# Table look-up of the feed-forward weights: products on POOL, sums on DVE

## The reference, cut to what matters

```python
xn = layernorm(x)                                     # (1, 1024, 256)
# attention: 16 heads of 128, causal, with a distance bias per head
q, k, v = split(xn @ qkv_w + qkv_b)
attn = softmax(q @ k.T + alibi_mask)
a = (attn @ v) @ out_w + out_b
# feed-forward: the weights are indices into a table of 16 values
gate = xn @ lut[gate_idx].T                           # gate_idx, up_idx: (688, 256)
up = xn @ lut[up_idx].T
f = (silu(gate) * up) @ lut[down_idx].T               # down_idx: (256, 688)
return x + a + f
```

## Time and profile before

| | us |
|---|---|
| median of 3 runs | 543.18 |
| lowest, highest | 539.96, 543.33 |
| profiled execution, device time | 543.26 |
| profiled execution, span of the core's instructions | 541.5 |
| PE busy | 493.8 (91%) |
| DVE busy | 414.2 (76%) |
| POOL busy | 403.6 (75%) |
| ACT busy | 360.9 (67%) |
| DMA queue that moves all data, share of 16 engines | 30.2% |

### The profile page before, as it was taken

How to read it: one execution, slowest core, us unless ns; L and a number is a source line. 1 busy time by engine, 2 the same in 40 slices (tenths; PEclk the granted TensorE clock), 3 DMA queues, 4 the chain that set the end, 5 groups by cost and what they waited for, 6 DMA issues and landing times.

```text
span 541.5 us, 9700 instructions
## 1 busy us (share of the span) xinstructions
PE 493.8 (91%) x2826; PEld 422.4 (78%) x2826; DVE 414.2 (76%) x1067; ACT 360.9 (67%) x657; POOL 403.6 (75%) x312
## 2 busy tenths in 40 slices
PE   7896797999889988998899989997999989789998
PEld 6785576898779876987689768986798779578897
DVE  6796988788888878888788987888788886543541
ACT  3575867687767867595959685877678766824430
POOL 5533989788978998798969897889789979921400
PEclk9997999999999999999999999999999999979999
DMA  8204243332514070606160524134331514000001
GB/s 285 87 0 101 62 98 103 73 91 53 146 44 116 13 186 4 156 0 161 38 144 16 119 80 113 47 79 120 70 90 43 119 38 104 0 1 2 0 21 58
DMA packets 18948, 41.65 MB, mean 77 GB/s; under 512 B 4848, under 2 KB 7024, under 8 KB 18800
## 3 DMA queue, kind: packets, MB, share of 16 engines
q1 hardware_dynamic: 18928, 41.40, 30.2%
HBM read 11.83 MB, written 1.05 MB: 24 GB/s over the span
## 4 chain that ended last, share of the span: by engine, by line
POOL 44%; PE 23%; issue 21%; DVE 7%; ACT 3%; DMA 1%; POOLq 0%; DVEq 0%; ACTq 0%
POOL p_t_lo L1125 17%; POOL w_ffn L1153 15%; POOL work L1118 5%; PE ps_u L447 5%; PE ps_u L449 4%; PE ps_u L448 4%; DVE term L958 3%; PE ps_s L447 2%; PE ps_s L448 2%; PE ps_s L449 2%; POOL v_w_lo L1102 2%; POOL pad L1117 2%; POOL qk_w_lo L1097 2%; ACT ctx_t_hi L721 1%; DVE ctx_t_lo L898 1%
## 5 line engine op out<-in xcount | busy, mean ns | idle before, releaser
L1153 POOL TENSOR_TENSOR w_ffn<-w_ffn,term 128x1088 f32<-128x1088 f32 x60 | 155.0, 2584 | 45.4 <-DVE term L958 45.4
L1125 POOL TENSOR_TENSOR p_t_lo<-p_t_lo,p_t_hi 128x1024 fp32r<-128x1024 f32 (+2 forms) x60 | 133.1, 2251 | 0.0
L738 ACT ACTIVATE work<-work,neg_max 128x128 f32<-128x128 f32 (+7 forms) x128 | 99.0, 773 | 24.1 <-DVE neg_max L937 22.1
L937 DVE CUSTOM_DVE_ANT_0 work<-ps_s,alibi 128x128 f32<-128x128 f32 (+7 forms) x128 | 95.8, 749 | 0.0
L447 PE MATMUL ps_u<-p_t_hi,v_hi 128*128 128x512 f32 x192 | 70.5, 367 | 17.7 <-POOL p_t_lo L1125 17.4
L975 DVE STREAM_TRANSPOSE blocks<-work 128x512 f32<-128x512 f32 x120 | 65.3, 582 | 11.6 <-ACT work L750 11.6
L447 PE MATMUL ps_s<-k_hi,q_hi 128*128 128x256 f32 (+2 forms) x192 | 67.3, 350 | 5.3 <-DVE neg_max L937 5.3
L958 DVE TENSOR_SCALAR term<-codes,entry,table 128x1088 f32<-128x1088 uint8 x60 | 65.8, 1096 | 4.3 <-POOL w_ffn L1153 4.3
L449 PE MATMUL ps_u<-p_t_hi,v_lo 128*128 128x512 f32 x192 | 67.2, 350 | 0.0
L448 PE MATMUL ps_u<-p_t_lo,v_hi 128*128 128x512 f32 x192 | 67.0, 349 | 0.0
L448 PE MATMUL ps_s<-k_lo,q_hi 128*128 128x256 f32 (+2 forms) x192 | 65.8, 343 | 0.0
(11 more groups left out here) (148 smaller groups left out, 1271.1 us busy)
## 6 DMA issues: line engine op xcount, KB each, us to landing
p_t_lo<-blocks SPq DMA_DIRECT2D x240, 116.0 KB, 2.3
qk_raw<-w_qk SPq DMA_DIRECT2D x16, 256.0 KB, 2.7
w_ffn<-idx SPq DMA_DIRECT2D x1, 2176.0 KB, 11.0
v_raw<-w_v SPq DMA_DIRECT2D x8, 256.0 KB, 3.5
o_raw<-w_o SPq DMA_DIRECT2D x8, 256.0 KB, 2.9
out<-acc SPq DMA_DIRECT2D x8, 128.0 KB, 1.7
acc<-x SPq DMA_DIRECT2D x2, 256.0 KB, 3.0
acc<-x SPq DMA_DIRECT2D x1, 512.0 KB, 5.0
```

The lines of the kernel that those rows point to most:

```text
L738: act.activation(slot(i), slot(i), ACT.Exp, bias=neg_max[:, col:col + 1], scale=-1.0, accum_out=row_sum[:, col:col + 1]).then_inc(exp_done, 1)
L937: dve.tensor_tensor_reduce(slot(i).rearrange("p (b c) -> p b c", b=banks), made_of, alibi[:, p, S - width:S].rearrange("p (b c) -> p b c", ...
L1125: pool.tensor_tensor(rows, rows.bitcast(F32), chunk_rows(0, chunk).bitcast(F32), ALU.subtract).then_inc(upper_lo, 1)
L1153: pool.tensor_tensor(piece, piece, term[:, :], ALU.add).then_inc(term_added, 1)
```

## The change

The two halves of a look-up change engines. The new `make_term` on POOL makes the product, the new `add_term` on DVE adds it to `w_ffn`; the head 0 path stays on DVE as `first_values`. POOL makes products in steps 0, 2, 4, 6, ahead of the splits of that step (but behind its `norm`); DVE adds at the end of steps 1, 3, 5, 7. Since POOL's scalar operands come from a tile at a fixed place, POOL first copies the head's two columns into `now`, once a head. The counts that ACT waits for in the last head are moved by one head, because head 0's parts count too.

```diff
-TERM_AT = (1, 3, 5, 7)
-SUM_AT = (1, 3, 6, 7)
+TERM_AT = (0, 2, 4, 6)
+SUM_AT = (1, 3, 5, 7)
...
+        now = sb("now", [P, 2, 2])
...
-                act.wait_ge(term_added, (HEADS - 2) * TERMS + reached)
+                act.wait_ge(term_added, (HEADS - 1) * TERMS + reached)
...
-                    act.wait_ge(term_added, (HEADS - 1) * TERMS)
+                    act.wait_ge(term_added, HEADS * TERMS)
...
-            def look_up(n, kind, p, part):
...
-                else:
-                    dve.wait_ge(term_added, n * (2 * TERMS) + (p - 1) * TERMS + part)
...
-                dve.tensor_scalar(target, codes[:, piece], column(entry, n, p), column(table, n, p),
-                                  ALU.is_equal, ALU.mult).then_inc(term_ready, 1)
+            def first_values(part):
...
+                dve.tensor_scalar(w_ffn[:, piece], codes[:, piece], entry[:, 0:1], table[:, 0:1],
+                                  ALU.is_equal, ALU.mult).then_inc(term_added, 1)
+
+            def add_term(n, p, part):
+
+                piece = w_ffn[:, part * LUT_PIECE:(part + 1) * LUT_PIECE]
+                dve.wait_ge(term_ready, n * (2 * TERMS) + (p - 1) * TERMS + part + 1)
+                dve.tensor_tensor(piece, piece, term[:, :], ALU.add).then_inc(term_added, 1)
...
-                        if i in TERM_AT:
-                            look_up(n, kind, p, TERM_AT.index(i))
+                        if i in SUM_AT:
+                            if kind == FIRST and p == 0:
+                                first_values(SUM_AT.index(i))
+                            else:
+                                add_term(n, p, SUM_AT.index(i))
...
+            def make_term(n, kind, p, part):
+
+                if part == 0:
+                    pool.tensor_copy(now[:, p, 0:1], column(entry, n, p)).then_inc(now_ready, 1)
+                    pool.tensor_copy(now[:, p, 1:2], column(table, n, p)).then_inc(now_ready, 1)
+                    pool.wait_ge(now_ready, n * 4 + p * 2)
+                    if kind == FIRST:
+                        pool.wait_ge(based, NT)
+                pool.wait_ge(term_added, n * (2 * TERMS) + p * TERMS + part)
+                if kind == FIRST:
+                    pool.wait_ge(codes_ready, TERMS)
+                pool.tensor_tensor(pad[:, 4 * NT + 1 + part:4 * NT + 2 + part], entry[:, 0:1], entry[:, 0:1], ALU.add)
+                pool.tensor_scalar(term[:, :], codes[:, part * LUT_PIECE:(part + 1) * LUT_PIECE],
+                                   now[:, p, 0:1], now[:, p, 1:2], ALU.is_equal, ALU.mult).then_inc(term_ready, 1)
...
+                        if i in TERM_AT and not (kind == FIRST and p == 0):
+                            make_term(n, kind, p, TERM_AT.index(i))
                         if i in (4, 5) and not (kind == FIRST and p == 0):
                             for chunk in (0, 1) if i == 4 else (2, 3):
                                 upper_lo_of(n, p, chunk)
...
-                        elif i in SUM_AT:
-                            part = SUM_AT.index(i)
-                            pool.wait_ge(term_ready, n * (2 * TERMS) + p * TERMS + part + 1)
-                            if kind != FIRST:
-                                pool.wait_ge(term_added, n * (2 * TERMS) + (p - 2) * TERMS + part + 1)
-                            piece = w_ffn[:, part * LUT_PIECE:(part + 1) * LUT_PIECE]
-                            pool.tensor_tensor(piece, piece, term[:, :], ALU.add).then_inc(term_added, 1)
```

More of the change, by code:

```diff
@@ L197, in block_ffn @@
         entry = sb("entry", [P, LUT])
-        pad = sb("pad", [P, 4 * NT + 1])
+        pad = sb("pad", [P, 4 * NT + 5])
         neg_max = sb("neg_max", [P, 2 * NT])
         row_sum = sb("row_sum", [P, 2 * NT])
+        now = sb("now", [P, 2, 2])
         inv_sum = sb("inv_sum", [P, 2 * NT])
@@ L233, in block_ffn @@
         h_padded = sem("h_padded")
-        based = sem("based")
+        based, now_ready = sem("based"), sem("now_ready")
         iota_done, made, normed, term_added = sem("iota_done"), sem("made"), sem("normed"), sem("term_added")
@@ L704, in _ @@
             act.wait_ge(made, 1)
-            act.activation(pad[:, 4 * NT:], eps[:, :], ACT.Sqrt)
+            act.activation(pad[:, 4 * NT:4 * NT + 1], eps[:, :], ACT.Sqrt)
             root(0)
@@ L711, in _ @@
             xn_hi_of(0, (1,))
-            act.activation(pad[:, 4 * NT:], eps[:, :], ACT.Exp)
+            act.activation(pad[:, 4 * NT:4 * NT + 1], eps[:, :], ACT.Exp)
             def hi_of(n, p, name, bank, no):
@@ L821, in h_hi_of @@
                 act.activation(h_tile(0, u)[rows, :], h_raw(u)[rows, :], ACT.Copy).then_inc(h_hi_done, 1)
-            act.activation(pad[:, 4 * NT:], eps[:, :], ACT.Silu)
+            act.activation(pad[:, 4 * NT:4 * NT + 1], eps[:, :], ACT.Silu)
             units = number(PAIRS - 1, LAST, 1, "pv0")
@@ L940, in mask @@
                                          neg_max[:, col:col + 1]).then_inc(scores_masked, 1)
-            def look_up(n, kind, p, part):
+            def first_values(part):
                 piece = slice(part * LUT_PIECE, (part + 1) * LUT_PIECE)
[L945 to L952, removed]
-                else:
-                    dve.wait_ge(term_added, n * (2 * TERMS) + (p - 1) * TERMS + part)
-                target = w_ffn[:, piece] if kind == FIRST and p == 0 else term[:, :]
-                if kind == FIRST and p == 0:
-                    dve.wait_ge(small_landed, 32)
-                dve.tensor_scalar(target, codes[:, piece], column(entry, n, p), column(table, n, p),
-                                  ALU.is_equal, ALU.mult).then_inc(term_ready, 1)
+                dve.wait_ge(idx_landed, 16)
+                dve.wait_ge(made, 6)
+                dve.tensor_copy(codes[:, piece], w_ffn[:, piece].bitcast(I32)).then_inc(codes_ready, 1)
+                dve.wait_ge(codes_ready, part + 1)
+                dve.wait_ge(small_landed, 32)
+                dve.tensor_scalar(w_ffn[:, piece], codes[:, piece], entry[:, 0:1], table[:, 0:1],
[4 more added lines that the diff above has]
+                dve.tensor_tensor(piece, piece, term[:, :], ALU.add).then_inc(term_added, 1)
             def invert(n, p, i):
```

## The result

The changed kernel takes 665.42 us (median of 4 executions, 662.13 to 667.05) and the kernel before, on the same chip, 542.89 us. The ratio is 1.2261, with a 95% interval of 1.2202 to 1.2320: 122.5 us slower. The profiled execution took 667.05 us, with a span of 665.3.

A forecast was written before the change was run, and what follows sets the result against it. PE was busiest and waited chiefly for POOL's splits and normalised tiles. Per pair, 0 for the p=0 head plus 0.4 us for p=1, seven times, gave 2.8 us more: 546 us (+0.5%), range 531 to 567.

The forecast's parts named there:

- The price of POOL's product: POOL's new one-input TENSOR_SCALAR of 1088 columns: taken as 1.15 us, from the norm and the select.
- The bound from above: Upper limit for POOL's product: 2.58 us, the time of the two-input sum it replaces.
- Rival 1: POOL's product is slow, so the kernel is slower: 566 us at 2.1 us a product, 576 at 2.58; chance 0.27.
- 3x a pair: Loss per pair of heads when POOL's product takes x us above 1.15, from three products ahead of the splits.
- The add on DVE: DVE's two-input add of 1088 float32 columns replaces its one-input product: 1.28 us, 0.44 more, 60 times.
- near 2.3 at step 5: Sign to look for: DVE's add at step 5, beside POOL's probability splits, takes near 2.3 us.
- The hold-ups: DVE's add and POOL's probability split delay each other: a hit split loses 0.45 us more than now.
- Head B's walk: Second head of a pair (p=0), followed through POOL and DVE: splits begin at 259.15 instead of 259.56, net 0.
- PE's slack: In the p=1 head POOL's last split ends 0.25 us ahead of PE's need; ending 0.65 later costs PE 0.4.
- nearly gone: Sign to look for: PE's wait for POOL's normalised tiles (L1118, 16.8 us before) almost vanishes.
- Rival 2: POOL and DVE get out of each other's way, so the kernel is faster: 533 or 530 us; chance 0.18.

The follow-up runs named there:

- the forecast case: Changed kernel with POOL's product from the second pair on made by multiply, multiply on float32 instead of is_equal and multiply: 555.75 us (ratio 1.0230).

## Why the prediction was wrong, point by point

- **The price of POOL's product.** This is the step that failed: "no row has that with uint8 and a comparison", and yet the two nearest rows were taken, 1.15 us, "because the two nearest rows agree on it". Measured 4.04. The norm is the mult*mult form, which is one of the quick pairs; the affine select is another instruction altogether. That the two agreed was chance. The bound from above failed as well: 2.58 was the time of a different instruction with two inputs, and says nothing on the one that replaces it. The Trainium skill's sentence weighed there (GPSIMD Engine Reference, "Performance pitfalls for Q7 kernels") gave an estimate of 1.84 or 0.93 us; the measured 4.04 agrees with neither.
- **Rival 1, a slow product.** Its mechanism and direction were right, at a chance of 0.27, but only up to the wrong bound. With x = 4.04 - 1.15 = 2.89 its "3x a pair" gives 7 x 8.7 = 61 us, hence 607. The kernel without full adds measured 601.4, but that closeness is luck: its pair is 64.1 us because POOL is full, busy 62.1 of them (256.00 to 320.10), not because three products stand in front of the splits. With real adds it is more: from 555.75 to 665.42 is 109.7 us, for 2.78 us more a product, or 109.7 / (7 x 2.78) = 5.6 products a pair.
- **A bound that was left out.** "Eight products of x in a pair must fit" could have been worked out: POOL was busy 49.6 of a pair's 57 us; less eight sums (20.6) and with eight products and `pad`s of 4.04 + 0.19 (33.8) it is 62.8 us, over the pair of 57.04 without any wait. From about 3.3 us a product POOL is full, and then each of the eight counts, not three. The run without full adds, at 62.1 busy, bears this out. Hold-ups take it to the 69.3 us seen in the windows (0.7 of them are the four copies).
- **The add on DVE.** Its own 1.28 us was right (1.28 to 1.29 undisturbed). The row in which the prediction saw the rule for two SBUF inputs borne out, 1.88 us against 0.84, is of an instruction with one, so it could not show that. The sign "near 2.3 at step 5" was not seen in the changed kernel, where it is 3.44: the add there is issued just behind the start of the splits, not in the middle of one.
- **The hold-ups.** The mechanism was right and its size too small: one hit of 0.45 us a head was counted. Even with the product at 1.26 us the hold-ups cost 17.0 us, of which 15.4 in the seven pairs, 2.2 a pair. Norms, `pad` and `o_w_lo` are hit too; in the changed kernel the mean of the 128-column norms is 1.35 us against 0.41, that of `o_w_lo` 2.34 against 1.30.
- **Head B's walk** (12.35 us from mask to splits, 12.3 measured in the forecast case) held; the sum over a pair did not (1.0 us instead of 0.4 in the forecast case), because the 0.44 us of the longer add at the end of head B were missing and the hits at the splits took 0.55 instead of 0.45. In the changed kernel nothing of the walk is left: head B's splits begin 21.6 us after its first mask (303.13 to 324.70).
- **PE's slack and clock.** That a later split costs PE in both heads was right: the waits after name it with 53.0 us. PE's wait for L1118, "nearly gone" in the prediction, rose from 10.4 to 45.5 us (matmuls, L592 after). The granted clock was 1.00 in every window of a pair's length before and is 0.87 to 0.97 in those after. So some of PE's matmuls ran at the lower of its two levels (1.2 and 2.4 GHz) in stretches after its waits: behind the 4.05 us before its first turn of head B the clock is 0.61 from 311 to 313 us and 0.54 from 313 to 315. This was not in my sum. PE is busy 534.2 us instead of 493.8 with the same 2826 matmuls, so it is at most some 40 of the 122 us; how much of that lies on the path was not separated.
- **Rival 2** (533 or 530 if they get out of each other's way) had no chance here: even with both parts cut to 8 columns the kernel takes 537.73, and its seven pairs give back 8.1 us where the rival asked for 10 with the look-up whole. A POOL that is busy 291.6 us instead of 403.6 is worth 1 to 1.5%.

## What to carry to other kernels

Before an operation goes to another engine, measure that very form there (operation pair, type, length) in an idle tail; a row of the same opcode with other operations is no price, and the time of the instruction that leaves is no upper bound. Then sum the engine's work in one period against the period: that tells from which price the engine is full, where a walk along the critical path stops being valid. When an experiment leaves a part of the loop in its old form, as the first pair here, compare the steady periods too. And where DVE and POOL work at the same time, count a DVE addition of two SBUF inputs twice, for itself and for what it stops; here most so right behind a product that POOL had just finished, where POOL's next instruction started 0.12 us after the add.

## What the runs showed of the hardware that I had not expected

- POOL's TENSOR_SCALAR of 1088 columns takes 1.25 us for mult*mult but 4.04 for is_equal*mult (uint8 and float32), subtract*mult and mult then max; a single mult takes 3.05, more than twice the pair. uint8 in place of float32 costs 0.45 us in the quick form (1.70, one row) and nothing that shows in the slow one.
- DVE runs the same is_equal*mult on uint8 in 0.84 us: the engine that the product left was nearly five times as quick at it.
- One input does not protect a DVE instruction as such: the one-input TENSOR_SCALAR of the look-up is held behind POOL's splits (2.98 and 3.01 us instead of 0.84), the one-input transpose in the same place is not (1.31). Which property decides was not tried.
- A hold-up can be many times the instruction's own length: the add of 8 columns (0.17 us elsewhere) takes 2.32 behind a split.
